# A state layer in 32 block steps instead of 8 batch steps, and the first attention unit's split rows moved ahead of the class tables

## The reference, cut to what matters

```python
h = h + ffn_fp4(layernorm(h))                  # second block
# third block (B=8, S=513, D=256, D_INNER=512, D_STATE=16)
xz = layernorm(h) @ w_in.T + b_in;  xc, z = split(xz)
xc = silu(causal_depthwise_conv4(xc) + b_conv)
x_dbl = xc @ w_xproj.T                         # 32 columns
delta = softplus(xc @ w_dt.T + b_dt)           # 16 columns
A  = exp(-abs(x_dbl[..., :16]) * delta)
Bx = x_dbl[..., 16:] * delta * xc[..., :16]
h_t = A_t * h_{t-1} + Bx_t                     # scan over time
y = pad(h_t, 512) * z;   h = h + y @ w_out.T
# fourth block: softmax attention (16 heads of 16) + top-2 of 8 experts
```

## Time and profile before

| | |
|---|---|
| median of 3 runs (lowest, highest) | 2006.7 us (2005.04, 2009.29) |
| the profiled execution's own time | 2004.92 us |
| its span | 2003.2 us |
| busy share: PE, DVE, ACT, POOL | 91%, 74%, 47%, 48% |
| state layer, end of last `add_h` to the first DMA of the next pass | 1119.6 to 1278.6 us, 159.0 us |
| in it: PE, DVE, ACT, POOL busy | 127.7, 116.0, 63.1, 25.5 us |
| attention, first to last instruction | 1564.4 us to the end |

### The profile page before, as it was taken

The page is one execution under the profiler, slowest core; times in us unless marked ns, Lnnn a source line. Parts: engine busy times, 40 slices in busy tenths (PEclk is TensorE's granted clock), DMA queues, the critical chain, the costliest instruction groups (busy, mean ns, idle before and its releaser), DMA issues. The chain is left out here.

```text
span 2003.2 us, 36356 instructions
## 1 busy us (share of the span) xinstructions
PE 1831.2 (91%) x10746; PEld 1205.2 (60%) x10746; DVE 1482.6 (74%) x4076; ACT 939.3 (47%) x2132; POOL 963.7 (48%) x1654
## 2 busy tenths in 40 slices
PE   6997997999899999899999699599889699999997
PEld 5886774444688888677777433288767333333332
DVE  3334896777477777699998388667789699999991
ACT  1112564566122122344444244345544488777777
POOL 3554564566333433233333111068844576666664
PEclk9997998999799999999999799699989799999999
DMA  4331568797100000597000200047877444444420
GB/s 135 115 115 32 151 177 202 159 181 153 48 1 1 1 1 1 215 414 292 1 1 1 64 9 11 27 122 200 207 227 232 99 100 105 107 97 95 94 70 28
DMA packets 241706, 215.01 MB, mean 107 GB/s; under 512 B 117210, under 2 KB 216188, under 8 KB 241404
## 3 DMA queue, kind: packets, MB, share of 16 engines
q1 hardware_dynamic: 227804, 183.51, 34.2%
q0 software_dynamic: 9408, 25.70, 4.1%
q10 hardware_dynamic: 4320, 3.70, 0.7%
HBM read 108.04 MB, written 103.12 MB: 105 GB/s over the span
## 5 line engine op out<-in xcount | busy, mean ns | idle before, releaser
L2932 ACT ACTIVATE attend_w<-ps 128x512 f32<-128x512 f32 x512 | 280.0, 598 | 78.0 <-PE ps L2792 71.2
L3160 DVE TENSOR_REDUCE attend_mx<-ps 128x1 f32<-128x512 f32 x448 | 281.8, 681 | 33.0 <-PE ps L2780 31.6
L2792 PE MATMUL ps<-keep_o,keep_x 99*128 99x512 bf16 x512 | 191.1, 382 | 9.3 <-DMA keep_o<-attend_nparts 6.9
L2780 PE MATMUL ps<-keep_x,keep_o 96*128 96x512 bf16 x448 | 172.6, 385 | 1.9 <-DVE attend_mx L3160 0.2
L987 POOL TENSOR_TENSOR keep_early<-keep_early,first_causal 128x128 f32<-128x128 f32 x256 | 111.2, 458 | 77.8 <-ACT keep_early L961 76.8
L1009 DVE SCALAR_TENSOR_TENSOR keep_early<-ps,first_causal 128x512 f32<-128x512 f32 (+3 forms) x256 | 111.3, 485 | 45.4 <-PE ps L901 44.5
L1215 PE MATMUL ps<-mlp_zT,keep_early 128*128 128x128 f32 x1056 | 128.5, 281 | 8.0 <-ACT mlp_zT L1257 8.0
L2810 PE MATMUL ps<-attend_w,keep_early 128*17 128x512 f32 x1024 | 135.5, 598 | 0.0
L961 ACT ACTIVATE keep_early<-ps 128x512 f32<-128x512 f32 (+3 forms) x256 | 97.0, 435 | 75.1 <-PE ps L901 74.6
L1215 PEld LDWEIGHTS ps<-mlp_zT,keep_early 128*128 128x128 f32 x1056 | 122.2, 194 | 16.0 <-ACT mlp_zT L1257 16.0
L2780 PEld LDWEIGHTS ps<-keep_x,keep_o 96*128 96x128 bf16 x448 | 43.7, 98 | 134.4 <-DVE attend_mx L3160 95.4
(11 more groups left out here) (409 smaller groups left out, 4488.7 us busy)
## 6 DMA issues: line engine op xcount, KB each, us to landing
sorted<-keep_x SPq DMA_DIRECT2D x3, 14720.0 KB, 75.1
tok_xin<-in_xk SPq DMA_DIRECT2D x64, 256.0 KB, 2.6
qk_parts<-qkv_parts SPq DMA_DIRECT2D x33, 384.0 KB, 3.2
qk_parts<-moe_parts SPq DMA_DIRECT2D x32, 384.0 KB
sorted<-moe_zn POOLq DMA_DIRECT2D x64, 128.0 KB, 3.0
moe_zs<-sorted SPq DMA_DIRECT2D x45, 128.0 KB, 3.0
keep_o<-qk_parts SPq DMA_DIRECT2D x14, 384.0 KB, 4.5
keep_x<-qk_parts SPq DMA_DIRECT2D x14, 384.0 KB, 5.7
```

What stands on the lines that cost most here:

```text
L2780: nc.tensor.matmul(ps[:, bank, :], qs[0:R, x.buf(0), h, t * P:(t + 1) * P], ks[0:R, x.buf(0), h, :], start=True, stop=True).then_inc(s_msc, 1)
L2792: nc.tensor.matmul(ps[:, SC + i % RING, :], ks[:, x.buf(2), HG * g + j, kt * P:(kt + 1) * P], qs[:, x.buf(2), HG * g + j, :], start=True, ...
L2932: nc.scalar.activation(w[:, j, kt % 2, :], ps[:, SC + (HG * k + j) % RING, :], ACT.Exp)\
L3160: nc.vector.tensor_reduce(mx[:, t, k:k + 1], ps[:, MX + (at + 1) % RING, :], AX, ALU.max)\
```

## The change

The state layer no longer goes by batch but in 32 steps g of a batch and a channel block (`GT = MI * B`). In step g, PE does `project(g)`, `turn(g + 6)`, every fourth step `gate`, and `states(g - 3)`; ACT does `silu(g - 3)`, `apply(g + 7)`, `take_zT(g + 5)` and `take_in(g)`; DVE does `convolve(g)` and the statistics of tile g + 11. There is no hardware loop any more.

- Normalizing moves from DVE to ACT (`apply`, an activation with a scale and a bias for each partition); POOL makes four small operations a tile instead of two.
- The last tap of the convolution moves from DVE to ACT: `take_in` reads the projection twice, once for `xb` and once, scaled, for `cv`. DVE keeps three `scalar_tensor_tensor`.
- The gate columns are computed as four tiles of 32 columns side by side in the array, 128 tokens each, and the states as two tiles of 64 columns, 256 tokens each (`tile_position`). The outputs lie in `[128, 128]` and `[128, 256]`, and SP writes them to the planes in 4 and 6 DMAs a batch instead of 1 and 3.
- The first five tiles (`FIRST`) are normalized already in `pass_fp4`: five `bn_stats` in steps 12 to 16 and five `bn_aggr` in step 17 on DVE, four small operations on POOL in step 18, one activation in each of steps 19 to 23 on ACT.
- Class tokens: nothing waits for their writes before the first batch; DVE makes only two bias vectors for them. At the end ACT issues three of the last six DMAs and one `Exp`.

In `pass_attend` SP issues rows 0 and 1 of the first unit's split maxima before the table `vb`, and ACT issues row 2 in step k = 5. POOL waits for `s_nm` before it splits the class values, and for `s_np` before `class_weights` of the first unit.

```diff
@@ pass_fp4
+                if 0 <= s - FIRST_AT - FIRST - 2 < FIRST:
+                    i = s - FIRST_AT - FIRST - 2
...
+                    nc.scalar.activation(first[:, i, :], env.h[:, i, :], ACT.Identity, bias=f_nb[:, i:i + 1],
+                                         scale=f_rs[:, i:i + 1])
...
+                if 0 <= s - FIRST_AT < FIRST:
+                    dve.wait_ge(s_h, s - FIRST_AT + 1)
+                    nc.vector.bn_stats(f_st[:, s - FIRST_AT, :], env.h[:, s - FIRST_AT, :]).then_inc(s_fbn, 1)
+                if s == FIRST_AT + FIRST:
...
+                    for i in range(FIRST):
+                        last = nc.vector.bn_aggr(f_mv[:, i, :], f_st[:, i, :])
@@ pass_ssm_in, PE
+            def gate(b):
+                pe.wait_ge(s_z16, b + 1)
+                for k in range(KD):
+                    for j in range(ZT):
+                        last = nc.tensor.matmul(ps[ZW * j:ZW * (j + 1), Z16, 0:P], w_in[:, k, DI:DI + ZW],
+                                                zT[:, b % 2, k, P * j:P * (j + 1)], start=(k == 0), stop=(k == KD - 1),
+                                                skip_group_check=True, tile_position=(0, ZW * j))
...
+            def states(g):
...
+                for j in range(PT):
+                    last = nc.tensor.matmul(ps[PW * j:PW * (j + 1), PR, 0:n], w_pr[:, m, :], xs[:, m, n * j:n * (j + 1)],
+                                            start=(m == 0), stop=(m == MI - 1), skip_group_check=True, tile_position=(0, PW * j))
...
+            for g in range(GT):
+                if g == 1:
+                    first_states()
+                project(g)
+                if g == 0:
+                    turn(FIRST)
+                if g + 6 < NT:
+                    turn(g + 6)
+                if g % MI == 1:
+                    gate(g // MI)
+                if g >= LAG:
+                    states(g - LAG)
@@ pass_ssm_in, ACT
-            act.wait_ge(s_o0, 48)
-            act.wait_ge(s_xb0, 1)
...
+            def take_in(g):
+                m = g % MI
+                act.wait_ge(s_in, MI + g + 1)
+                past(act, s_cv, g - MI + 1)
+                nc.scalar.activation(xb[:, m, H:H + S], ps[:, X0 + m, :], ACT.Identity, bias=col(env, "b_in", m)).then_inc(s_xb, 1)
+                past(act, s_xs, MI + g - MI + 1 if g >= MI else 0)
+                nc.scalar.activation(cv[:, m, :], ps[:, X0 + m, :], ACT.Identity, bias=b_tap[:, m:m + 1], scale=last_tap(m))\
+                    .then_inc(s_tap, 1)
...
+            for g in range(GT + LAG):
+                if g >= LAG:
+                    silu(g - LAG)
+                if g >= LAG + MI and (g - LAG) % MI == 0:
+                    take_states((g - LAG) // MI - 1)
+                if g < GT:
+                    if FIRST + 2 <= g + 7 < NT:
+                        apply(g + 7)
+                    if g + 5 < NT:
+                        take_zT(g + 5)
+                    take_in(g)
@@ pass_ssm_in, DVE
+                for j in range(DC - 1):
+                    ins = nc.vector.scalar_tensor_tensor(cv[:, m, :], xb[:, m, j:j + S], col(env, "w_conv", DC * m + j), cv[:, m, :],
+                                                         ALU.mult, ALU.add)
...
+            for s in range(FIRST, AHEAD):
+                stats(s)
+            for g in range(GT):
+                convolve(g)
+                if g + AHEAD < NT:
+                    stats(g + AHEAD)
@@ pass_attend, SP
+            def first_rows(c0, c1):
+                sp.wait_ge(s_np, 1)
+                sp.sem_inc(s_took, 1)
+                for c in range(c0, c1):
+                    sp.dma_start(qs[R + c:R + c + 1, 0, :, :], nparts[NR:NR + HALF, c, :]).then_inc(s_nmd[0], 16)
...
+                first_rows(0, 2)
                 sp.wait_ge(s_dparts, 96)
```

More of the change, by code:

```diff
@@ L1606, in pass_ssm_in @@
     H = DC - 1
+    ZT, PT = P // ZW, P // PW
+    GT = MI * B
+    LAG, AHEAD = 3, 11
+    RING = 4
     with a.ctx:
@@ L1666, in _ @@
+            sp.wait_ge(s_oz, 16 * ZT * B)
+            sp.wait_ge(s_ox, 16 * B)
+            sp.wait_ge(s_op, 48 * PT * B)
         @block.tensor
@@ new lines, in first_project, with first_gate @@
+            def first_project(m):
+                if m == 0:
+                    pe.wait_ge(s_zT, 1)
+                for k in range(KD):
+                    last = nc.tensor.matmul(ps[:, X0 + m, 0:B], w_in[:, k, m * P:(m + 1) * P], zT0[:, k, :],
+                                            start=(k == 0), stop=(k == KD - 1))
+                last.then_inc(s_in, 1)
+            def first_gate():
+                for k in range(KD):
+                    last = nc.tensor.matmul(ps[0:ZW, Z16, 0:B], w_in[:, k, DI:DI + ZW], zT0[:, k, :],
@@ L1708, in _, with project @@
-            turn(-1)
-            project(-1)
-            states(-1)
-            turn(0)
-            project(0)
-            with pe.Fori(1, B) as b:
-                turn(b)
-                project(b)
-                states(b - 1)
-            states(B - 1)
+                    last = nc.tensor.matmul(ps[0:PW, PR, 0:B], w_pr[:, m, :], xs0[:, m, :], start=(m == 0), stop=(m == MI - 1))
+                last.then_inc(s_st, MI)
+            def project(g):
+                b, m = g // MI, g % MI
+                if m == 0:
+                    pe.wait_ge(s_zT, 1 + TB * (b + 1))
+                pe.wait_ge(*((s_xs, m + 1) if b == 0 else (s_tap, g - MI + 1)))
+                for k in range(KD):
+                    last = nc.tensor.matmul(ps[:, X0 + m, :], w_in[:, k, m * P:(m + 1) * P], zT[:, b % 2, k, :],
+                                            start=(k == 0), stop=(k == KD - 1))
+                last.then_inc(s_in, 1)
@@ new lines, in _ @@
+            turn(0)
+            turn(1)
+            for m in range(MI):
+                first_project(m)
+                if m + 2 < FIRST:
+                    turn(m + 2)
+            first_gate()
+            for g in range(GT):
[10 more added lines that the diff above has]
+                    states(g - LAG)
@@ L1719, in _ @@
+            for g in range(GT - LAG, GT):
+                states(g)
         @block.scalar
@@ new lines, in take_states @@
+            def take_states(b):
+                act.wait_ge(s_st, MI * (b + 2))
+                past(act, s_op, 48 * PT * b)
+                nc.scalar.copy(pr[:, :], ps[:, PR, 0:S // PT]).then_inc(s_prs, 1)
+            take_zT(0)
+            take_zT(1)
+            take_zT(2)
+            for m in range(MI):
+                first_in(m)
+                if m + 3 < FIRST:
+                    take_zT(m + 3)
+            act.wait_ge(s_zin, 1)
+            nc.scalar.activation(z0[:, :], ps[0:ZW, Z16, 0:B], ACT.Identity, bias=b_z[0:ZW, :]).then_inc(s_z16, 1)
@@ L2734, in _ @@
             for x in slots():
-                if x.has(1):
-                    u = x.half(1)
+                u = x.half(1)
+                if x.s == 1:
+                    heads.load(sp, io, 1, 1, 3)
+                elif x.has(1):
                     sp.wait_ge(s_np, x.n(1) + 1)
```

351 lines of the change are left out of this document (182 added, 169 removed).

## The result

The changed kernel takes 1958.2 us (median of 4 runs, 1954.03 to 1960.18), the kernel before 2006.0 beside it: ratio 0.9756, 95% interval 0.9735 to 0.9778. The forecast was 1954 (1947 to 1971). The profiled execution took 1959.98, its span is 1958.2. Two more series of five gave 1955.6 and 1955.8.

The account below looks back on a forecast made before the run. DVE was taken to bound the state layer at 15.78 us a batch, PE having about 3 us left. State layer -49.2, fp4 pass +0.5, attention -3.5: -52.2 us, giving 1952.7, stated as 1954 us (1947 to 1971).

Parts of the forecast that it names:

- The three engines' sums: State layer, one step: DVE 2.82 us, PE 2.84, ACT 2.76, from added instruction times.
- The step taken, 2.95 and 2.65: State layer: 2.95 us for the first 25 steps, 2.65 for the last six, since engines with little slack never fit perfectly.
- Tiles: States on PE: two 64-column tiles run side by side, 0.43 us streaming plus 0.22 for entering and leaving.
- Rival A: State layer: the 64-column tiles run one after the other, PE sets a 3.3 us step, +11, 1965 us; 14%.
- rival B: State layer: ACT becomes the bound at 3.2 us a step, +8, 1962 us; 14%.
- rival D: State layer: PE stays at 1.2 GHz, a step takes 5.7 us, 2039 us, slower than before; 3%.
- Front, 1131.5 forecast: State layer's start: after transposes, class projections and the first real projection, the first convolution starts at 1131.5 us.
- Tail, 5.8 forecast: State layer's end: 5.8 us from the last convolution to the next pass instead of 7.0.
- six issues on two queues take what three on one took: State layer's end: the last six transfers' issues on two queues take 1.77 us, as three on one did.
- Attention, -3.5 forecast: Attention's start: rows sent earlier start scores 5.0 us earlier; with the table then late, gain 1.5 to 5.0, taken as 3.5.
- A gain of this kind lasts, because PE is busy from here to the end: Attention: the 3.5 us gained at its start stay to the end.
- Rival C: Attention's start: rows arrive early for nothing, the reader waits for the class table, gain 0 to 1.5, 1957 us; 8%.

Follow-up runs that it names:

- the last two kernels of the experiments: The changed kernel with the states as one untiled matmul per block, 1962.9 us; the changed kernel with the convolution's last tap back on DVE, 1962.1 us.

## Why the prediction was right, and where it was not

- *The three engines' sums:* PE 2.84 forecast, 2.86 measured; DVE 2.82 and 2.77; ACT 2.76 with the scaled read at 0.65 and the normalizing at 0.50, measured 0.66 and 0.50, which gives 2.8. Sums of start-to-start distances held to 3%. In PE's sum some of this is luck: projection and transposes cost 1.82 and 0.31 where 1.77 and 0.26 were forecast, states and gate 0.58 and 0.57 where both stood at 0.65.
- *The step taken, 2.95 and 2.65:* from the second convolution (1138.00) to the 28th (1211.78) are 26 steps of 2.84, the last four are 2.64. The margin for an imperfect fit wasn't needed: a convolution has two steps' room before its SiLU is due, and over 76 us PE never idled. This was 0.11 us too much in 24 steps, 2.7 us; but the second convolution came 4.82 us after the first, 1.9 more than a step, and two steps forecast at 2.65 took 2.84, so that the 31 steps ended 0.5 us under the forecast.
- *Tiles:* 0.58 us for the states against 0.65 forecast (0.43 + 0.22). Rival A, 0.86 us of streaming alone, is refuted by these 0.58, and the untiled form was 0.42 us dearer. On what the Trainium skill says there (TensorEngine Tiling (Array Packing), Tiling Modes and Overview): the trace agrees that two 64-column tiles work in parallel, 0.58 us for what takes 1.00 untiled. That changing the tiling mode costs extra isn't seen in these rows: what lies over the streaming is 0.58 - 0.43 = 0.15 us in the tiled form and 1.00 - 0.86 = 0.14 in the untiled one.
- *ACT as the bound* (rival B) and *the low clock* (rival D): neither. ACT waited 4.6 us for PE from 1144 to 1220, and the clock was 1.00.
- *Front, 1131.5 forecast, 1133.2 measured:* 1.3 us came from the passes ahead. The half clock lasted over a second projection, which is why the second convolution came late: in the executions where it ended earlier, the second convolution followed the first by 2.80 us. Counted from the layer's own start the front took 11.1 us against 10.7, but by luck: PE started the first real projection 5.3 us after its first transpose instead of 6.4, since the class matmuls were priced too high, and the first convolution came 2.3 us after that projection's end (1130.84) instead of about 1 (1131.5 less 1127.2 and 3.4), since ACT's reads stood behind the copy that waited for the transposes.
- *Tail, 5.8 forecast, 6.95 measured:* the failed step is "six issues on two queues take what three on one took". SP had five others to issue first; I had counted them for the buffers and not for the end. That is 0.8 us of the 1.15; in the kernel with the tap on DVE, where SP was free, the end took 6.2 us. The rest is SP's three issues (2.06 us instead of 1.77) and the last states with their copy, 1.0 us shorter than before and not 1.2.
- *fp4 pass:* +0.5 forecast, 0.0 measured.
- *Attention, -3.5 forecast, +1.3 measured:* this is the largest miss, and the step that failed is "A gain of this kind lasts, because PE is busy from here to the end". The wait itself was as priced (the table's reader at 1580.0 to 1583.5 forecast by the clock of before, 1581.4 measured), and an attention that gives back what its start gained was named as what would show the forecast wrong. The first score's 6.3 us went in four parts: PE's second wait (2.04 us), a second stretch of half clock behind it (18.0 to 21.4 us in; one group of values took 1.91 us instead of 1.05), waits for DVE and ACT 25 to 27 us in, and waits for DVE at the units' ends (0.75 us at 37.2, 0.62 at 46.5), where the next units' rows leave no earlier than before. The first two don't suffice: the last two kernels of the experiments had both and were still 2.2 us ahead at the ninth group (46.9 us). What the last two hang on stays open. PE's share of 97% (405.5 of 418 us from 1585 on, kernel before) hid how closely the other engines follow: once PE was ahead, it waited for them. The 1.3 us over the kernel before isn't the part's own, since the attention took 440.1 and 440.4 us without it. Rival C had the result at 1957 us, but by another way: in it the table's reader gains at most 1.5 us, and here it ran 3.7 us earlier and the lead was lost behind it.

Sum of the misses in the profiled execution: +1.3 and +0.7 (passes ahead of and behind the layer), +0.4 (front), -0.5 (steps), +1.2 (tail), +4.8 (attention) and -0.5 (fp4), together +7.4; by spans it is 1958.2 against 1951.0 (2003.2 less 52.2), 7.2. This execution lies at the upper end of the series; by the median the forecast was 4 us low, and 2 us by the two later series.

The best version run is the changed kernel without its attention part, 1953.4 us in both series, about 2 us below the changed kernel, at the edge of what can be told.

## What to carry to other kernels

When a loop's work is spread over engines, add up start-to-start distances for each engine; if each item has a step or two of room, the step is the largest sum, without a margin for the fit. Before counting a lead as kept, find what the stage's next handover waits for: here a table was needed 6 us after the rows, and the units' ends hung on DVE, so moving one transfer ahead of another only changed which of them PE waited for. Count a queue's other issues at the end of a pass as well as in its steady part.

## What the runs showed of the hardware

- The granted clock of 0.50 at the layer's front lasted 3.4, 6.8 or 13.7 us in executions of the same code (state layers of 104.7, 106.3 and 109.6 us), with PE busy all the time. That is 5 us, more than most parts of this change are worth. The profiled executions with the longest stretch were the longer ones of their kernel: 1960.0 us against 1956.6 and 1956.4 with the attention part, 1958.6 against 1954.2 without it. So it may explain much of the spread of 1952.5 to 1960.2 us; the other executions have no profile.
- In the attention PE's clock was 1.00 while PE waited for the table (1533 to 1535 us), and fell to 0.50 at 1536.1, 1 us after PE had begun to work again.
- Three transfers issued on ACT's queue beside six of the table on SP's could be read 7.0 us after the last of them was issued; issued ahead of the table (two by SP, one by ACT) they could be read 1.3 us after SP's second (1527.26 to 1528.59).
- A scaled read of PSUM costs ACT 0.77 us for 512 columns in place of 0.69, 0.08 us.
